# Layer 1's first queries and keys made beside the last tile of layer 0's mixture

## What is computed

```
x = x + L0_attn(layernorm(x))
x = x + L0_ffn(layernorm(x))      # mixture: per output channel, the two greatest of 8 experts
x = x + L1_attn(layernorm(x))     # 16 query heads, 4 key/value heads of 128; w_qkv, w_proj
x = x + L1_ffn(layernorm(x))      # gate, up, down in 4-bit weights

# L0_ffn
logits = (h @ router_w.T + router_b).reshape(T, O, E); probs = softmax(logits)
w, sel = top_k(probs, 2); w = w / sum(w); c = zeros(T, E).at[sel].add(w)
final = einsum('te,teo->to', c, einsum('th,eoh->teo', h, expert_w) + expert_b)

# L1_attn: the attention runs over axis 1 of an (s, b) layout, so over the 4 sequences' tokens at one position
qkv = einsum('sbh,ph->sbp', x, w_qkv).reshape(s, b, 4, 6 * 128)   # per kv head: 4 queries, key, value
```

## Time and profile before

| what | value |
|---|---|
| median of 3 runs | 1158.56 us (1158.07 to 1158.87) |
| profiled execution, its own time | 1155.52 us |
| its span, first to last instruction | 1153.8 us |
| mean granted TensorE clock | 0.941 |
| busy: PE, DVE, ACT, POOL | 981.7, 854.3, 498.0, 307.6 us |

### The profile page before, as it was taken

The page is one execution under the profiler, slowest core; times in us unless marked ns, Lnnn a source line. Parts: engine busy times, 40 slices in busy tenths (PEclk is TensorE's granted clock), DMA queues, the critical chain, the costliest instruction groups (busy, mean ns, idle before and its releaser), DMA issues. The chain is left out here.

```text
span 1153.8 us, 19875 instructions
## 1 busy us (share of the span) xinstructions
PE 981.7 (85%) x6885; PEld 579.3 (50%) x6960; DVE 854.3 (74%) x1556; ACT 498.0 (43%) x972; POOL 307.6 (27%) x337
## 2 busy tenths in 40 slices
PE   3698989897789778797649799999978999999997
PEld 1444545454446344454214366575846555656564
DVE  5677776651999999999977875858762776777766
ACT  2154444453465464564624433416131444444443
POOL 3234343441352432423321121304044400000000
PEclk9799999998899989798769999999988999999999
DMA  6622222200101001001000010101011000000000
GB/s 176 118 75 77 72 82 67 74 2 4 44 0 47 1 1 45 0 1 46 1 17 3 10 30 8 31 2 32 8 36 39 20 1 19 1 18 0 19 1 19
DMA packets 37087, 35.87 MB, mean 31 GB/s; under 512 B 8584, under 2 KB 33416, under 8 KB 37008
## 3 DMA queue, kind: packets, MB, share of 16 engines
q1 hardware_dynamic: 35728, 33.79, 10.5%
q10 hardware_dynamic: 1280, 1.05, 0.7%
HBM read 27.28 MB, written 6.29 MB: 29 GB/s over the span
## 5 line engine op out<-in xcount | busy, mean ns | idle before, releaser
L883 DVE TENSOR_REDUCE bm<-ps 128x4 f32<-128x512 f32 x160 | 102.1, 684 | 32.6 <-PE ps L603 30.5
L782 ACT ACTIVATE pt<-ps 128x1024 f32<-128x1024 f32 (+1 forms) x96 | 82.0, 882 | 70.9 <-PE ps L679 70.2
L2011 ACT ACTIVATE g<-ps 128x512 f32<-128x512 f32 x64 | 38.2, 597 | 134.4 <-PE ps L1958 107.4
L2061 DVE SCALAR_TENSOR_TENSOR g<-g,ps 128x512 f32<-128x512 f32 x64 | 44.0, 687 | 54.7 <-ACT g L2011 54.5
L1753 DVE TENSOR_TENSOR qk_lo<-ps,qk_hi 128x512 bf16<-128x512 f32 x80 | 54.8, 686 | 40.1 <-ACT qk_hi L1646 34.1
L599 PE MATMUL ps<-ks,qs 96*128 96x512 bf16 (+3 forms) x256 | 68.7, 323 | 11.9 <-DMA ks<-scratch_k 7.6
L156 POOL TENSOR_TENSOR mag_w<-stage 128x512 f32<-128x512 fp8e4 x24 | 26.4, 1100 | 191.2 <-DVE stage L143 191.2
L1515 PE MATMUL ps<-wp_hi,oT_hi 128*128 128x256 bf16 x256 | 71.2, 278 | 5.4 <-DVE oT_lo L1746 5.4
L547 POOL TENSOR_SCALAR_AFFINE_SELECT pt<-pt 128x256 f32<-128x256 f32 (+1 forms) x96 | 45.9, 484 | 109.4 <-ACT pt L782 108.9
L1974 PE MATMUL ps<-ew_hi,it_hi 128*128 128x256 bf16 x256 | 69.8, 273 | 6.0 <-DVE it_lo L2077 6.0
L1646 ACT ACTIVATE qk_hi<-ps 128x512 bf16<-128x512 f32 x80 | 48.1, 603 | 55.0 <-PE ps L1515 55.0
(11 more groups left out here) (272 smaller groups left out, 2803.5 us busy)
## 6 DMA issues: line engine op xcount, KB each, us to landing
qs<-scratch_q SPq DMA_DIRECT2D x64, 64.0 KB, 2.6
ks<-scratch_k SPq DMA_DIRECT2D x48, 64.0 KB, 2.5
q_next<-in_w_qkv SPq DMA_DIRECT2D x4, 768.0 KB, 5.0
X<-in_x SPq DMA_DIRECT2D x4, 512.0 KB, 7.0
w_next<-in_router_w SPq DMA_DIRECT2D x4, 512.0 KB, 3.9
w_next<-in_expert_w SPq DMA_DIRECT2D x4, 512.0 KB, 4.7
p_next<-in_w_proj SPq DMA_DIRECT2D x4, 512.0 KB, 5.9
out<-X SPq DMA_DIRECT2D x8, 256.0 KB, 2.3
```

The lines of the kernel that those rows point to most:

```text
L782: act.activation(pt[kt][:, heads[0]:heads[-1] + 1, :], src, ACT.Exp).then_inc(s_exp, 1)
L883: ins = dve.tensor_reduce(bm[:, 2 * g + i // 5, 4 * (i % 5):4 * (i % 5) + 4], src.rearrange("p (k q) -> p k q", k=4), AX_X, ALU.max)
```

## The change

15 of the 20 tiles of queries and keys of group 0 are completed inside the mixture's block, beside its last token tile, and the matmuls of four more run there too. The details:

- `next_queries_keys` is new on PE, after the last batch: 19 tiles of 6 matmuls into banks 0 to 3 in turn. From the fifth on a tile waits for the low part of the tile four before it. The last four are left in PSUM.
- ACT makes the high parts of tiles 0 to 14 (`next_high`), the eight token weights of the last tile between them.
- On DVE, the last tile's work is a generator of 30 steps (`last_tile`), and `interleave` puts two of them behind each of 15 low parts: `wq_lo`, the statistics of group 1, the eight `weigh` steps, `wp_lo`, the statistics of group 2, and the normalisation of group 1. `xT_lo` is made one tile earlier.
- POOL builds `mask` and `same` and takes group 1's root beside the last tile.
- The new `qk` parts of kv heads 0 to 2 lie in the buffers of the tournament (now one tile, `tourney`) and of the first logits (`first_lg`), which stay allocated; that of kv head 3 has its own.
- In layer 1, PE makes one tile (19), ACT and DVE five high and low parts, and the scores follow. Group 3's statistics move into round 0. The root of groups 2 and 3 is taken apart.

```diff
+                def next_queries_keys():
+                    pe.wait_ge(s_xhi2, KC)
+                    pe.wait_ge(s_xlo2, KC)
+                    for m in range(TILES1 + 4):
+                        if m % (HQ + 1) == 0:
+                            q = m // (HQ + 1)
+                            pe.wait_ge(s_next, NEXT * q + 1)
+                        if m >= 4:
+                            pe.wait_ge(s_qklo2, m - 3)
+                        w = GROUP * (m // (HQ + 1)) + HD1 * (m % (HQ + 1))
+                        n = 0
+                        for c in range(KC):
+                            for a, x in ((glob["wq_hi"], xT_hi), (glob["wq_hi"], xT_lo), (glob["wq_lo"], xT_hi)):
+                                mm = pe.matmul(bank(m % 4), a[:, c, w:w + P], x[:, c, :], start=(n == 0), stop=(n == 3 * KC - 1))
+                                n += 1
+                        mm.then_inc(s_qk2, 1)
...
                 all_batches(pe, batch)
+                next_queries_keys()
...
-                        if after:
+                        if after and not (last and t == 2):
                             token_weights(n + 1, after[1])
+                        if last and t == 3:
+                            next_high(0)
+                            act.wait_ge(s_kept, n + 1)
+                            for m in range(1, TILES1):
+                                if m <= E:
+                                    token_weight(m - 1, t)
+                                next_high(m)
...
-                        if last and t == 1:
-                            next_root()
+                        if last and t == 3:
+                            next_mask()
+                        if last and t in (1, 3):
+                            next_root(t // 2)
...
+                def last_tile(b, n, t):
+
+                    weights_low(b, 0)
+                    yield
+                    yield from next_statistics(1)
+                    yield from weighing(b, n, t)
+                    weights_low(b, 1)
+                    yield
+                    yield from next_statistics(2)
+                    yield from next_normalised(1)
...
                         if last and t == 3:
-                            next_low()
+                            interleave(next_queries_keys_low(), TILES1, last_tile(b, n, t), 2 + 2 * 2 * B + E + B)
+                            continue
...
+                        if last and t == 2:
+                            next_low()
...
-                queries_keys(0, range(NM))
+                pe.sem_inc(s_qk, NM - 1)
+                queries_keys(0, (NM - 1,))
...
-                queries_keys_high(0, range(NM))
+                act.sem_inc(s_qkhi, TILES1)
+                queries_keys_high(0, range(TILES1, NM))
...
-                dve.wait_ge(const, 3 + P // 8)
-                tiles, rest = queries_keys_low(0), chain(statistics(1), statistics(2), statistics(3))
-                interleave(tiles, NM - 6, rest, 6 * B)
-                for _ in tiles:
+                dve.sem_inc(s_qklo, TILES1)
+                dve.wait_ge(const, 1)
+                for _ in queries_keys_low(0, TILES1):
                     pass
-                dve.wait_ge(s_rstd, 4)
-                normalised(1)
...
+                    if g == 0:
+                        tiles, last_rows = queries_keys_low(1), statistics(3)
...
+                        if g == 0:
+                            main, steps = chain(main, islice(last_rows, 2)), steps + 2
```

More of the change, by code:

```diff
@@ L79, in interleave, with first_queries_keys @@
             done += 1
+def first_queries_keys(glob):
+    n = (HQ + 1) * S
+    room = [a[:, :].bitcast(BF16)[:, n * i:n * (i + 1)] for a, count in ((glob["tourney"], 4), (glob["first_lg"], 2))
+            for i in range(count)]
+    parts = [a.rearrange("p (h t) -> p h t", h=HQ + 1) for a in room]
+    return parts[0::2], parts[1::2]
 E = 8
@@ L967, in layer0_mixture @@
         far, wt = st.sb("far", [P, E, D], F32), st.sb("wt", [P, E, D], F32)
-        s4, h4 = st.sb("s4", [P, 4, D], F32), st.sb("h4", [P, 4, D], F32)
-        h2, a2, c2 = (st.sb(n, [P, 2, D], F32) for n in ("h2", "a2", "c2"))
-        m1, n1, c1, m2, both, mid = (st.sb(n, [P, D], F32) for n in ("m1", "n1", "c1", "m2", "both", "mid"))
+        room = glob["tourney"]
+        s4, h4 = (room[:, a:a + 4 * D].rearrange("p (e o) -> p e o", e=4) for a in (0, 4 * D))
+        h2, a2, c2 = (room[:, a:a + 2 * D].rearrange("p (e o) -> p e o", e=2) for a in (8 * D, 10 * D, 12 * D))
+        m1, n1, c1, m2, both, mid = (room[:, D * i:D * (i + 1)] for i in range(14, 20))
         cw = [st.sb(f"cw{n}", [P, E], F32) for n in range(2)]
@@ L1180, in token_weights, with token_weight, next_high @@
                     for e in range(E):
[L1181 to L1182 removed]
+                        token_weight(e, t)
+                def token_weight(e, t):
+                    act.activation(far[:, e, :], far[:, e, :], ACT.Copy, accum_out=cw[t % 2][:, e:e + 1]).then_inc(s_cw, 1)
+                def next_high(m):
+                    act.wait_ge(s_qk2, m + 1)
+                    act.activation(qk_hi[m // (HQ + 1)][:, m % (HQ + 1), :], bank(m % 4), ACT.Copy).then_inc(s_qkhi2, 1)
                 act.sem_inc(s_xhi, 4)
@@ L1294, in weigh, with weighing @@
                 def weigh(b, n, t):
+                    for _ in weighing(b, n, t):
+                        pass
+                def weighing(b, n, t):
                     c_t = cw[t % 2]
@@ L1360, in batch @@
                             masked(n + 1)
-                        if t == 2:
+                        if t == 2 and not last:
                             weights_low(b, 0)
@@ L1393, in layer1_attention @@
         xT_hi, xT_lo = ([glob[n][:, :, :], spare(w)] for n, w in (("xT_hi", "ew_hi"), ("xT_lo", "ew_lo")))
-        qk_hi = st.sb("qk1_hi", [P, KV, HQ + 1, S], BF16)
-        qk_lo = st.sb("qk1_lo", [P, KV, HQ + 1, S], BF16)
+        qk_hi, qk_lo = ([*parts, st.sb(f"qk1_{n}", [P, HQ + 1, S], BF16)]
+                        for n, parts in zip(("hi", "lo"), first_queries_keys(glob)))
         v = st.sb("v1", [P, NB, KV, HD1], F32)
-        mask = st.sb("mask1", [P, T8], F32)
-        same = st.sb("same1", [P, 8], F32)
+        mask, same = glob["mask"], glob["same"]
         mx = [st.sb(f"mx1_{n}", [P, H1], F32) for n in range(NB)]
@@ L1479, in _, with root @@
             def _(pool):
[L1480 removed]
+                pool.sem_inc(s_rstd, 4)
                 pool.sem_inc(const, 1)
[L1482 to L1494 removed]
+                def root(g):
+                    wait_alone(pool, s_mv, B * g + B, passed_pool)
+                    pool.tensor_scalar(rstd[:, g, :], mv[:, g, :, 1], EPS, None, ALU.add).then_inc(s_rstd, 1)
+                    wait_alone(pool, s_rstd, 2 * g + 1, passed_pool)
+                    pool.tensor_tensor(rstd[:, g, :], rstd[:, g, :], half[:, g, :], ALU.pow).then_inc(s_rstd, 1)
+                root(2)
                 for g in range(G):
                     unit_weights(pool, g)
+                    if g == 0:
+                        root(3)
                     if g == 1:
@@ L1534, in queries_keys @@
                     for m in tiles:
-                        before = [k for k in range(m) if QK_BANK[k] == QK_BANK[m]]
+                        before = [k for k in range(m) if qk_bank(g, k) == qk_bank(g, m)]
                         if before:
@@ L1542, in queries_keys @@
                         w = GROUP * (m // (HQ + 1)) + HD1 * (m % (HQ + 1))
-                        three(bank(QK_BANK[m]),
+                        three(bank(qk_bank(g, m)),
                               [lambda c: wq_hi[:, c, w:w + P], lambda c: wq_lo[:, c, w:w + P]],
@@ L1747, in outputs_lo, with queries_keys_low @@
                         yield
-                def queries_keys_low(g):
-                    for m in range(NM):
+                def queries_keys_low(g, first=0):
+                    for m in range(first, NM):
                         dve.wait_ge(s_qkhi, NM * g + m + 1)
                         k, h = m // (HQ + 1), m % (HQ + 1)
-                        dve.tensor_tensor(qk_lo[:, k, h, :], bank(QK_BANK[m]), qk_hi[:, k, h, :],
+                        dve.tensor_tensor(qk_lo[k][:, h, :], bank(qk_bank(g, m)), qk_hi[k][:, h, :],
                                           ALU.subtract).then_inc(s_qklo, 1)
```

99 lines of the change are left out of this document (59 added, 40 removed).

## The result

| | before | changed |
|---|---|---|
| median of the first comparison | 1158.56 us (1158.07 to 1158.87) | 1145.87 us (1145.40 to 1147.66) |
| ratio, 95% interval | | 0.9901 [0.9888, 0.9913] |
| profiled execution, its span | 1155.52, 1153.8 us | 1145.40, 1143.7 us |
| median of all executions of this study | 1156.89 us (78 of them, 1153.02 to 1159.62) | 1146.78 us (17, 1144.92 to 1150.93) |

The change made the kernel faster by 12.7 us in the first comparison, by 10.1 us between the two profiled executions, and by 10.1 us between the medians of all executions.

What follows compares the result with a forecast made beforehand. It took DVE (mixture) and then PE (layer 1) to bound the kernel one after the other, split by the barrier. Scores 8.5 us earlier less 1.1 us in round 0 gave 7.4 us: 1158.56 to 1151.2 us, range 1148.6 to 1155.2.

Steps and rivals of the forecast that it cites:

- PE's 19 tiles: In the mixture, behind the last experts' matmul: 19 tiles without a gap at full clock, 24.6 us.
- The 0.3 us for tile 13: In the mixture: tile 13's matmuls wait for low part 9 on DVE, 0.3 us added, bounds 0 and 3.7.
- half clock at tile 19: Layer 1's one tile: PE restarts at half clock after 2.7 us idle, 2.78 us for the tile instead of 1.51.
- the third rival: Layer 1's tile 19 runs at full clock: 1.3 us less, 1149.9 us; chance 0.16.
- The border: Between mixture and layer 1: 0.9 us to ACT's first instruction, then 1.38 us until PE starts tile 19.
- the 1.2 us for the constants: Layer 1 before tile 2: about 1.2 of the 8.5 us gained come from constants taken off the path.
- Statistics in round 0: Group 3's 1.65 us of DVE statistics, moved into round 0, cost 1.1 us there, bounds 0 and 1.65.
- the 0.26 ahead of round 0: One statistics instruction ahead of the low part PE waits for: 0.33 less 0.07 us, 0.26 lost.
- POOL holding DVE: Mixture: POOL's mask and root instructions hold DVE's large ones, up to 3.7 us, 1154.9 us; rival, chance 0.18.
- Half clock through the mixture's tiles: PE's clock stays at half through the tiles, 24 us more, 1175 us; rival, chance 0.04.
- Decoded weights late: The round behind waits for decoded weights and the gain is given back, about 1158 us; rival, chance 0.05.
- The base: Whole kernel: the forecast starts from the runs' median, 1158.56 us, 3.04 us above the profiled execution.

Runs made afterwards that it cites:

- tiles5: Changed kernel with 5 instead of 15 tiles completed in the mixture, four more left in PSUM, the others back in layer 1: medians 1157.06 and 1157.07 us.
- tile19_late: Changed kernel with PE waiting, before tile 19, for the low part of tile 18 in place of tile 15: median 1149.41 us.
- tiles10: Changed kernel with 10 instead of 15 tiles completed in the mixture, four more left in PSUM, the others in layer 1: 1153.46 us, ratio 0.9976.
- const_early: Kernel before with one part alone, POOL building `mask` and `same` in the mixture: median 1154.68 us, ratio 0.9979.
- stats3_early: Changed kernel with group 3's statistics moved from round 0 to the end of the mixture: median 1147.62 us.

## Why the prediction missed its range

The mechanism was right and held step by step; the miss is one of sizes: 2.7 us in the kernel's gain, 1.7 in the base, and 0.9 by which the first comparison's median of the changed kernel lies below its level.

- **PE's 19 tiles.** Right. They start 8.04 us behind the mark of stage A (7.85 by the prediction) and have no gap. The 0.3 us for tile 13 did not come: DVE's list, laid out with rows of before, was a little too long.
- **The step that failed: half clock at tile 19.** "After 2.26 us of idling it restarted at half clock; after 1.23 us it did not. I take half clock." The tile ran at full clock, 1.49 us from its start to ACT's copy instead of 2.78, in all three profiles of the changed kernel, behind 2.15 us. The 2.26 rested on one row of one execution, and before's second profile has full clock at that very place, behind 2.05 us. Of all 14 profiles three have half clock there (before's first, the changed kernel's second, the first of tiles5) and eleven full clock, always behind 2.0 to 2.05 us of waiting, 2.2 to 2.3 where the first matmul is not on record. So no rule could be read from that row. The length of the idle time does not decide elsewhere either: tile19_late has 3.94 us and full clock at the start, tiles5 2.15 us and half clock. These rows and tiles10's would fit a rule by what PE did before the wait: 24.8 us of tiles without a gap in the changed kernel, waits of 0.81 and 2.86 us among them in tiles5. The border of the last block speaks against a gapless run as the reason, since PE runs there for some 23 us without a gap and the clock goes both ways; it was not tried by itself, and what decides stays open. The term is worth 1.27 us, and the third rival had it. The arithmetic of the idle time was off too: its own sum has PE's last matmul end at 613.7 and tile 19 start at 616.0, which is 2.3 us and not 2.7, and either lies above both rows and not between them, as the third rival says.
- **The border.** 0.60 us from PE's last matmul (612.86) to ACT's first instruction (613.46), 0.9 predicted; from there to tile 19 it took 1.54, not 1.38. All terms together: 0.2 later at the start, then 0.3 (DVE), 1.27 (clock) and 0.3 - 0.16 (border) earlier, 1.5 us. Stage A gained 10.0, 8.5 predicted. Of the 1.2 us for the constants, const_early shows 0.89.
- **Behind the scores.** Statistics in round 0: 1.1 us predicted, 1.27 by stats3_early. Of the 0.26 ahead of round 0 nothing was seen in B (17.76 against 17.78): the first transposition now comes 0.91 us behind the scores and not 1.15, because the normalisation left this stretch, and that gave as much back. "The last two cost nothing" was wrong by 0.2. In the profile of the changed kernel 8.9 us are left at that point.
- **The rivals.** POOL holding DVE: `far` and the masking took 2.32 and 2.29, so at most 0.1 us; it was POOL that was held, and its 10.22 us (4.71 in before) were in nobody's way. Half clock through the mixture's tiles: not seen. Decoded weights late: D is before's when the statistics are out of it.
- **The rest of the gain.** From the mark of A to the end of D the changed kernel's first profile is 8.9 us ahead of before's first profile and 10.3 ahead of its second, which had 1.45 us more half clock in C. The 10.1 us between the first two profiles are 8.9, the 0.74 ahead of the mark and 0.7 in E, less 0.2 in the last block; the 0.74 and the 0.7 are not the change's as far as the rows show. All pairs of profiles together give 8.9 to 11.0 for these stages; that the medians too lie 10.1 apart is in keeping with that, and no more is shown.
- **The base.** The prediction took the median of three executions, 1158.56, 3.04 us above the profiled one, for the kernel's level. Over 78 executions that level is 1156.89. With the prediction's 7.4 and this level the forecast would have been 1149.5; with its base and the measured gain of 10.1 it would have been 1148.5, just below its range; with both it is 1146.8, the level of the changed kernel. So it took both misses to bring the time well outside. A range made only of mechanisms left out the spread of the executions, 6 us.

Open: E is 201.3, 202.0 and 201.5 in the three profiles with the statistics moved and 202.5 to 202.7 in the changed kernel's, while before had 203.4 and 202.5; but const_early, where they were not moved, has 201.8. Some 0.2 us of such differences are a first matmul that is not on record. The instructions of E are the same, and it was not tried what makes the difference.

## What to carry to other kernels

Work moved onto an idle engine pays the difference between what the later block loses and what the earlier one gains in length (26.6 less 16.6 us here), and most where its step stays unbroken: the same tiles with a few waits between them cost the waits, and in the three profiles with fewer tiles there was half clock further on as well, in a place that the edit never touched. Do not take the clock behind a short wait from one row of one execution: profile the kernel twice and see whether the row comes back. Judge an edit of 1 us by the stages of the trace that repeat between executions, cut at marks on one engine, and not by a median of five; and before a median of three becomes the base of a forecast, look at how far the profiled execution lies from it, for here that distance was 3.04 us, and the median turned out 1.7 us above the kernel's level. When a wait is removed, ask first what it had been hiding: behind PE's 2.15 us before tile 19 stood DVE's copies, and 0.57 us were all there was to win.

## What the hardware showed that was not expected

The clock and the idle time come apart. After 3.94 us of idling four matmuls still ran at full clock, and the fall came inside the work; behind 0.71 us it fell in three profiles (tiles5 twice, tiles10) and not in the changed kernel's three. And behind 2.02 and 2.05 us one and the same kernel, the changed one, restarted at full clock in one execution and at half clock in another, though PE had run for 23 us and more without a gap before it in both.

POOL beside DVE: sixteen small instructions of POOL took 10.22 us from first to last between DVE's large ones, and 4.71 in before (busy 9.2 and 3.7 us). DVE's were at most 0.06 us longer than alone. The time sits in three of the sixteen, 2.15, 2.26 and 1.82 us, which end 0.09 us behind `far`, the masking and `wq_lo`; the others take about 0.24. All sixteen, and the one beside the masking (which runs from 586.61 to 588.90):

```profile
583.91 10.22 POOL L1069 TENSOR_SCALAR_AFFINE_SELECT mask<-mask 128x32 f32<-128x32 f32 x16
586.73 2.26 POOL L1069 TENSOR_SCALAR_AFFINE_SELECT mask<-mask 128x32 f32<-128x32 f32 x1
```

In before and in const_early `far` took 2.88 us, since it began while POOL's 128x2048 instruction still ran (until 584.97 in const_early, and `far` ended 2.14 behind that); in the changed kernel `xT_lo` stands first and `far` takes 2.32. So the one that comes second is held until the other's instruction ends, on either side, and short ones cost a long one next to nothing. By the section "Who interferes with whom" of the Trainium skill's page "SBUF — State Buffer", the port pair that VectorE and GpSimd share is an exclusive lock, and the order of issue decides who blocks; the trace agrees.
